# Mixture-of-experts layer: weighted slot results added by accumulating gathers, and a last shared phase that turns its inner rows through DRAM

## What is computed

```python
scores = softmax(xt @ Wg.T)                      # 16 experts, 4 groups; the best 2 groups stay
topi = top_k(masked, 4)                          # 4 experts a token
weights = take_along_axis(scores, topi)
h = silu(xt @ W1[e].T) * (xt @ W3[e].T)          # inner size 352
y = sum over e of (h @ W2[e].T) * weight of e
z = silu(xt @ Ws1.T) * (xt @ Ws3.T) @ Ws2.T      # shared expert, inner size 704
return y + z
```

## Time and profile before

| | |
|---|---|
| runs | 923.56, 919.63, 924.39 us, median 923.56 |
| span of the profiled execution | 919.3 us; no time of its own is listed beside it |
| last shared phase | about 810 to 919 us of the span |
| granted TensorE clock | 0.998 of full speed over the span |
| moved by DMA | 218.97 MB, 238 GB/s over the span |

### The profile page before, as it was taken

How to read it: one execution, slowest core, us unless ns; L and a number is a source line. 1 busy time by engine, 2 the same in 40 slices (tenths; PEclk the granted TensorE clock), 3 DMA queues, 4 the chain that set the end, 5 groups by cost and what they waited for, 6 DMA issues and landing times.

```text
span 919.3 us, 19365 instructions
## 1 busy us (share of the span) xinstructions
PE 899.9 (98%) x4962; PEld 806.1 (88%) x4963; DVE 557.9 (61%) x1105; ACT 332.0 (36%) x708; POOL 494.3 (54%) x346
## 2 busy tenths in 40 slices
PE   8999998899989999999999999999999999999998
PEld 5777887687889999999999999999999999989997
DVE  6656767888896644544444444444444444459997
ACT  4556554354324322333333333333333333332221
POOL 1127777874167764434646664456666643136772
PEclk9999999999999999999999999999999999999999
DMA  6829996665569956878778776788777755588984
GB/s 214 264 106 385 388 403 251 230 189 172 184 227 297 308 206 207 243 205 247 245 235 252 248 246 203 237 244 258 248 251 249 248 170 158 163 231 241 275 254 144
DMA packets 180649, 218.97 MB, mean 238 GB/s; under 512 B 56576, under 2 KB 124160, under 8 KB 180224
## 3 DMA queue, kind: packets, MB, share of 16 engines
q1 hardware_dynamic: 118080, 123.49, 41.9%
q0 software_dynamic: 20816, 79.44, 26.1%
q10 hardware_dynamic: 41712, 15.54, 6.3%
HBM read 127.38 MB, written 91.03 MB: 238 GB/s over the span
## 4 chain that ended last, share of the span: by engine, by line
PE 80%; DVE 9%; issue 4%; ACT 3%; DMA 3%; ACTq 0%; DVEq 0%; POOL 0%; SPq 0%; POOLq 0%
PE ps L1170 15%; PE ps L1171 15%; PE ps L1172 15%; PE ps L1222 8%; PE ps L1224 8%; PE ps L1223 8%; PE ps L1019 2%; PE ps L1035 2%; PE ps L966 1%; DVE st L1469 1%; DVE res L1467 1%; PE ps L1055 1%; PE ps L1057 1%; PE ps L1056 1%; DVE st L1284 1%
## 5 line engine op out<-in xcount | busy, mean ns | idle before, releaser
L1170 PE MATMUL ps<-whi,xhi 128*128 (+1 forms) x888 | 288.8, 325 | 1.2 <-issue 0.6
L1172 PE MATMUL ps<-whi,xlo 128*128 (+1 forms) x888 | 286.7, 323 | 0.0
L1171 PE MATMUL ps<-wlo,xhi 128*128 (+1 forms) x888 | 286.7, 323 | 0.0
L1544 DVE TENSOR_TENSOR hrow<-ps,sg 128x352 f32<-128x352 f32 x95 | 49.7, 523 | 214.1 <-ACT sg L838 214.1
L1170 PEld LDWEIGHTS ps<-whi,xhi 128*128 128x128 f32 x888 | 167.7, 189 | 6.1 <-issue 1.3
L1171 PEld LDWEIGHTS ps<-wlo,xhi 128*128 128x128 f32 x888 | 167.7, 189 | 3.9
L1172 PEld LDWEIGHTS ps<-whi,xlo 128*128 128x128 f32 x888 | 167.3, 188 | 0.0
L838 ACT ACTIVATE sg<-ps 128x352 f32<-128x352 f32 x111 | 51.5, 464 | 268.1 <-PE ps L1172 268.0
L845 ACT ACTIVATE xhi<-ps 128x512 fp32r<-128x512 f32 x112 | 66.9, 597 | 145.8 <-DVE ps L1505 145.7
L566 POOL TENSOR_TENSOR wlo<-raw,whi 128x2816 fp32r<-128x2816 f32 x16 | 100.7, 6291 | 2.4 <-POOL whi L564 0.9
L658 POOL DMA_INDIRECT raw<-yslot_d,sloti x64 | 67.7, 1058 | 57.7 <-DMA yslot_d<-ysb 22.6
(11 more groups left out here) (201 smaller groups left out, 1583.4 us busy)
## 6 DMA issues: line engine op xcount, KB each, us to landing
raw<-wexp_in POOLq DMA_DIRECT2D x18, 2176.0 KB, 11.1
xslot_d<-zero SPq DMA_DIRECT2D x10, 2048.0 KB, 21.6
xg<-xslot_d SPq DMA_DIRECT2D x320, 64.0 KB, 2.8
yslot_d<-ysb SPq DMA_DIRECT2D x80, 256.0 KB, 2.4
h_d<-hrow ACTq DMA_DIRECT2D x79, 192.0 KB, 3.0
hblk<-h_d SPq DMA_DIRECT2D x79, 192.0 KB, 2.5
xg<-xn_d SPq DMA_DIRECT2D x128, 64.0 KB, 3.7
xq<-x_in SPq DMA_DIRECT2D x16, 256.0 KB, 3.3
```

The costliest lines, as they stand in the source:

```text
L1170: pe.matmul(ps[:, bank, 0:INTER], xh, wh, start=(k == 0), stop=False)
L1171: pe.matmul(ps[:, bank, 0:INTER], xh, wl, start=False, stop=False)
L1172: mm = pe.matmul(ps[:, bank, 0:INTER], xl, wh, start=False, stop=(k == KT - 1))
```

## The change

It has three parts.

1. **Weights move into the slots.** The softmax over all 16 experts is worked out at the start of the first shared phase (`prob`). Rows of xslot_d grow from 512 to 528 numbers (SROW): the scattered row carries the token's 16 probabilities, brought into `scat` by a second small load. In the expert phase SP loads the 16 probabilities of each tile's slots (`load_w`), and ScalarE's `y_evac` scales by the column of the tile's expert, which it reads from the packed table, so that yslot_d holds weighted results.
2. **Gathers accumulate.** The 64 gathers of the last phase have `compute_op=ALU.add` and go to x1 directly. They are ordered in four groups of four tiles, choice by choice; each waits for the previous choice of its tile. gath, `combine` and the semaphore comb go. `add_last` stands one step later and waits for all four gathers of its tile.
3. **Last shared phase as expert tiles.** Tiles 0 to 14 store the inner row to h_d (`store_last_h`), load it (`load_last_h`) and turn it on VectorE (`last_h_turn`); the down product is two tiles behind. Tile 15 alone is still transposed by TensorE (`tr_last_h`). The gate product alternates between two PSUM banks here too, and the phase is written out without a loop. The weights of the second shared half are laid out as the experts' are; for tile 15 VectorE writes the inner row in that order by two instructions.

```diff
+SROW = D + E
-LAG, PACE = 1, 9
-        xslot_d = nc.dram_tensor("xslot_d", [NR * P, D], F32, kind="Internal").ap()
+        xslot_d = nc.dram_tensor("xslot_d", [NR * P, SROW], F32, kind="Internal").ap()
         def gate_bank(base, p):
-            return 7 if base == NT and p else 2
+            return 7 if base >= NT and p else 2
...
             def load_scat(t, r, turn):
-                sp.dma_start(scat[:, r, :], rows(xn_d, t)).then_inc(scat_loaded[r], 16)
+                sp.dma_start(scat[:, r, 0:D], rows(xn_d, t)).then_inc(scat_loaded[r], 16)
+                if type(t) is not int or t >= XR:
+                    sp.dma_start(scat[:, r, D:SROW], prob[:, bass.ds(t, 1), :]).then_inc(scat_loaded[r], 16)
+                elif t == XR - 1:
+                    sp.wait_ge(rt_prob, 1)
+                    for i in range(XR):
+                        sp.dma_start(scat[:, i, D:SROW], prob[:, i, :]).then_inc(scat_loaded[i], 16)
...
+            def load_w(t, r, turn):
+                if type(t) is int and t == NR - 1:
+                    return
+                if type(t) is not int or t >= XG:
+                    sp.wait_ge(y_out, 2 + NT + t - XG + 1)
+                sp.dma_start(wslot[:, r, 2:2 + E], rows(xslot_d, t)[:, D:SROW]).then_inc(w_loaded[r], 16)
...
-            stream(sp, [(NR, True, [(-1, load_h), (XG + 1, load_slots), (-3, store_y)], None),
-                        (NT, False, [(0, None), (XG + 1, load_tile(NT + NR, xn_d)), (-4, store_out)], None)], XG)
+            stream(sp, [(NR, True, [(-1, load_h), (XG + 1, load_slots), (-3, store_y), (1, load_w)], None),
+                        (NT, False, [(-1, load_last_h), (XG + 1, load_tile(NT + NR, xn_d)), (-5, store_out), (0, None)], None)], XG)
...
-            for t in range(NT):
-                if 1 <= t < GR:
-                    pool.wait_ge(gathered[t - 1], 16 * TOPK)
-                if t >= GR:
-                    pool.wait_ge(mm1, 2 + NT + NR + t - 2)
-                    pool.wait_ge(comb, TOPK * (t - GR + 1))
+            for first in range(0, NT, GR):
                 for k in range(TOPK):
-                    pool.indirect_dma_start(
-                        out=gath[:, t % GR, k, :], out_offset=None, in_=yslot_d,
-                        in_offset=bass.IndirectOffsetOnAxis(ap=sloti[:, t * TOPK + k:t * TOPK + k + 1], axis=0)).then_inc(gathered[t % GR], 16)
+                    for t in range(first, first + GR):
+                        if first or k:
+                            pool.wait_ge(gathered[t % GR], 16 * TOPK * (t // GR) + 16 * k)
+                        pool.indirect_dma_start(
+                            out=x1[:, t, :], out_offset=None, in_=yslot_d,
+                            in_offset=bass.IndirectOffsetOnAxis(ap=sloti[:, t * TOPK + k:t * TOPK + k + 1], axis=0),
+                            compute_op=ALU.add).then_inc(gathered[t % GR], 16)
...
-                act.activation(ysb[:, p, :], ps[:, 5 + p, :], ACT.Copy).then_inc(y_out, 1)
+                act.wait_ge(w_loaded[r], 16 * (turn + 1))
+                act.activation(ysb[:, p, :], ps[:, 5 + p, :], ACT.Identity, scale=wslot[:, r, bass.ds(expert(t, r), 1)]).then_inc(y_out, 1)
...
-                         (NT, True, [(0, by_two(silu_g(NT + NR))), (0, None), (-1, by_two(h_high(NT + NR))), (2, by_two(x_high(NT + NR))), (0, None), (0, None)], None)], XG)
+                         (NT, False, [(0, by_two(silu_g(NT + NR))), (0, store_last_h), (0, None), (2, by_two(x_high(NT + NR))), (-2, by_two(h_high(NT + NR))), (0, None)], None)], XG)
...
-                        (NT, True, [(0, tr_h(NT + NR)), (-1, down(NT + NR, last)), (2, up(NT + NR, last))], None)], XG)
+                        (NT, False, [(-1, tr_last_h), (-2, down(NT + NR, last)), (2, up(NT + NR, last))], None)], XG)
...
+            r_shifted()
             dve.wait_ge(h_pad, 1)
             h_mult(0)(0, 0, 0)
...
             x_turn(0)(2, 2, 0)
+            r_softmax()
...
             def add_last(t, r, turn):
                 p = r % 2
                 dve.wait_ge(mm2, NT + NR + t + 1)
-                if issued["comb"]:
-                    dve.wait_ge(comb, issued["comb"])
+                dve.wait_ge(gathered[r], 16 * TOPK * (turn + 1))
...
-                         (NT, False, [(0, h_row(NT + NR)), (0, combine(0)), (0, None), (2, x_turn(NT + NR)), (-1, h_low(NT + NR)), (0, combine(1)),
-                                      (2, x_low(NT + NR)), (-2, add_last), (0, combine(2)), (0, combine(3))], None)], XG)
+                         (NT, False, [(0, h_row(NT + NR)), (0, None), (0, None), (2, x_turn(NT + NR)), (-2, last_h_turn), (2, x_low(NT + NR)),
+                                      (-2, h_low(NT + NR)), (-3, add_last)], None)], XG)
```

More of the change, by code:

```diff
@@ L322, in xattn_moe @@
         gathered = [sem(f"gathered{r}") for r in range(GR)]
-        comb = sem("comb")
+        w_loaded = [sem(f"w_loaded{r}") for r in range(XG)]
         out_stored = [sem(f"out_stored{p}") for p in range(2)]
@@ L409, in fn @@
                     sp.wait_ge(x_tr, base + t + 1)
-                    blocks = rows(src, t).rearrange("(c i) (q n) -> i q c n", i=Q, q=NQ)
+                    blocks = rows(src, t)[:, 0:D].rearrange("(c i) (q n) -> i q c n", i=Q, q=NQ)
                     for q in range(NQ):
@@ L873, in _ @@
             silu_g(0)(0, 0, 0)
+            act.wait_ge(rt_low, 1)
+            act.activation(prob[:, :, :], prob[:, :, :], ACT.Exp).then_inc(rt_exp, 1)
             def h_high(base):
@@ L888, in h_high, with load_words, expert, y_evac @@
                 return fn
-            def y_evac(t, p, half):
+            words = []
+            def load_words(j):
+                words[:] = [act.value_load(packed[0:1, bass.ds(j, 1)], min_val=0, max_val=32 ** XG - 1)]
+            def expert(t, r):
+                if type(t) is int:
+                    return act.value_load(order[0:1, t:t + 1], min_val=2, max_val=E + 1)
+                return words[0] // 32 ** ((r + 2) % XG) % 32
+            def y_evac(t, r, turn):
+                p, half = r % 2, 2 * turn + r // 2
+                if type(t) is int and t == 0:
+                    act.wait_ge(rt_done, 1)
                 act.wait_ge(mm2, NT + t + 1)
@@ L913, in second_high, with silu_again @@
                         first_high(1)(i, p, half)
-            def exponents(t, p, half):
-                if type(t) is int and t == 5:
-                    act.wait_ge(rt_low, 1)
-                    act.activation(score[:, :, :], score[:, :, :], ACT.Exp).then_inc(rt_exp, 1)
-                    act.activation(top8f[:, :, 0:TOPK], top8f[:, :, 0:TOPK], ACT.Exp).then_inc(rt_exp, 1)
+            def silu_again(t, p, half):
+                if type(t) is int and t == 0:
+                    act.activation(silu_warm[:, :], const[:, C_EPS:C_EPS + 1], ACT.Silu).then_inc(warm, 1)
             def expert_high(t, p, half):
@@ L1160, in fn @@
                     for m in halves:
-                        if base == NT and m:
+                        if base >= NT and m:
                             pe.wait_ge(h_ready, base + t)
@@ L1233, in fn, with tr_last_h @@
                     pe.wait_ge(h_lo, base + t)
-                    transposes(ps[:, 4, :], hrow[:, p % 2, :] if base else hx[:, :], IC, h_tr)
+                    transposes(ps[:, 4, :], hx[:, :], IC, h_tr)
                 return fn
+            def tr_last_h(t, r, turn):
+                if t < NT - 1:
+                    return
+                pe.wait_ge(h_ready, NT + NR + t + 1)
+                pe.wait_ge(h_lo, NT + NR + t)
+                transposes(ps[:, 4, :], hrow[:, r % 2, :], IC, h_tr)
             words = []
@@ L1775, in _ @@
             x_turn(0)(2, 2, 0)
-            issued = {"comb": 0, "y_out": 2 + NT}
+            r_softmax()
             def add_last(t, r, turn):
@@ L1786, in add_last @@
                 dve.tensor_tensor(x1[:, t:t + 1, :], x1[:, t:t + 1, :], ps[:, 5 + p:6 + p, :], ALU.add).then_inc(y_out, 1)
-                issued["y_out"] = 2 + NT + NR + t + 1
-            def combine(quarter):
-                def fn(s, r, turn):
-                    begin, end = (max(0, min(TOPK * NT, ((4 * u + v) - 4 * LAG) * PACE // 8)) for u, v in ((s, quarter), (s, quarter + 1)))
-                    for n in range(begin, end):
-                        t, k = n // TOPK, n % TOPK
-                        if k == 0:
-                            dve.wait_ge(gathered[t % GR], 16 * TOPK * (t // GR + 1))
-                        dve.wait_ge(y_out, issued["y_out"])
-                        if n:
-                            dve.wait_ge(comb, n)
-                        dve.scalar_tensor_tensor(x1[:, t:t + 1, :], gath[:, t % GR, k:k + 1, :], top8[:, t:t + 1, k],
-                                                 x1[:, t:t + 1, :], ALU.mult, ALU.add).then_inc(comb, 1)
-                        issued["comb"] += 1
-                return fn
             def first_row(t, r, turn):
```

80 lines of the change are left out of this document (52 added, 28 removed).

## The result

The changed kernel takes 951.37 us (median of five runs, 949.67 to 958.45) against 923.56: 1.0325 times as long, interval 1.0288 to 1.0361. That is slower, close to the 955.0 forecast and inside the range.

What follows compares the result with a forecast made beforehand. TensorE bounds the old kernel, DMA engines the changed last shared phase. Span 919.3 - 6.5 (TensorE) + 37.9 (gathers end last) = 950.7, plus 4.3 from span to time: 955 us; range 914 to 988.

Steps and rivals of the forecast that it cites:

- TensorE's gain of 0.43 us a tile: Last shared phase: 15 of 16 tiles run as expert tiles do, without PE transposes, 6.5 us less.
- The tail does not grow: End of last shared phase: tile 15's work unchanged, one more down product covers its latency; nothing added.
- Price of an adding gather: Last shared phase: 21.6 engine-us each against 14.4 plain, by bytes, half as much again; bounds 14.4 and 28.8.
- the rival of two passes: Last shared phase: both operands pass the DMA engine in turn, 28.8 engine-us a gather, 986 us; chance 0.18.
- 94% as the most that the DMA engines give: Last shared phase: busy share taken from the scatters' stretch, making 138.8 us of DMA work last 147.6 us.
- The mechanism: Last shared phase: full DMA engines make gathers end last, +37.9 us; VectorE waits for gathers at additions, TensorE gets holes.
- the change doesn't do what it says: Last shared phase: rival of inner rows waiting for their round trip, only with full DMA engines; counted inside the forecast.
- POOL's pace no longer sets the rate: Last shared phase: a round of four gathers lasts one landing plus 0.3 us of issue; POOL's time 5 us a round.
- forecast idle time of 4 us a round: Last shared phase: sign that POOL stands idle some 4 us in each round of gathers.
- Expert phase at 0 (0 to 5): Expert phase: weight load and longer slot rows cost nothing, or 0 to 5 us if weight-load bursts exceed the cover.
- First shared phase at 0 (at worst +2): Front of first shared phase: the early softmax fits into existing waits, 0 in all, at worst +2 us.
- From span to time: Whole kernel: 4.3 us added to the span, as the earlier runs' median lies above the profiled span.

Runs made afterwards that it cites:

- pe_turn: Changed kernel with the last shared phase's inner rows transposed by TensorE and the down product one tile behind, as before, adding gathers kept; 938.12 us, ratio 1.0180.
- half_adds: Changed kernel with only two of each tile's four adding gathers (32 in all), the other two choices missing from the output; 935.58 us, ratio 1.0150.
- no_gathers: Changed kernel with no gathers and no wait for them in the final addition, routed part missing from the output; 923.13 us, ratio 1.0017.
- turn_only: Kernel before with only the last phase's inner rows turned through DRAM and VectorE; plain gathers, weighted and added by VectorE; 929.78 us, ratio 1.0077.
- plain_gathers: Changed kernel with its 64 gathers not adding, written to a buffer in the same order with the same waits; 925.30 us, ratio 1.0027.

## Why the prediction was right, point by point

- **TensorE's gain of 0.43 us a tile: right.** Tile 95 to 110 went from 93.9 to 86.6 us without gathers, 7.3 us for 15 tiles where 6.5 was forecast. In the changed kernel the same stretch takes 106.7, so the gain is buried under the waits.
- **"The tail does not grow": wrong.** Without any gather the stretch from tile 110 to the end went from 9.7 to 12.5 us, and to 20.8 with the adding ones. The forecast had every tile's latency covered by a down product and overlooked that tile 14's round trip is on the path once the up products are over.
- **Price of an adding gather: right in kind, 8% low.** 23.6 engine-us, forecast 21.6. The second read, from which the price was worked out, is seen in no view. The Trainium skill (Collectives: The Full Stack, "The bandwidth ceiling: the fold count and why AG ≠ RS ≠ AR") states its rule for reduce-scatter in a ring; applied here it would have doubled the plain price. The traces have 23.6 / 14.4 = 1.64, so the rival of two passes, 986 us, fell.
- **94% as the most that the DMA engines give: wrong.** The share was 1.09 to 1.13 for 120 us. The measured work from 800 us on, gathers 1512 and hardware queues 977 engine-us (29.7% and 9.2%), is 269 more than the 2220 forecast (a part of the hardware queues' 139 more are expert tiles that now lie inside the window). A first gather 11.9 us later than forecast (811.78), a stretch to the last landing of 134.5 us instead of 147.6, and 10.6 us behind that landing instead of 3.2: 950.7 + 11.9 - 13.1 + 7.4 = 956.9. The hit of the total is owed in good part to errors that cancel.
- **The mechanism: half right.** That DMA work of the adding gathers decides, and that TensorE gets holes, was right. That the damage comes as gathers ending last, with VectorE waiting at the additions of tiles 4, 8 and 12, was wrong for this kernel: 0.5 us of such waits, and the chain does not end with a gather. It is right for pe_turn, at those very tiles. So 13.1 of the 25.9 us of the last phase are the gathers' late stream, as forecast, though POOL's pace has most part in it, and 12.8 came by the inner rows' round trip, which the forecast had folded into its rival "the change doesn't do what it says" and priced at nothing of its own. half_adds shows the error in the reasoning: the loss accrues while gathers run and needs no overrun at the end (over no_gathers 15.2 us with 32 of them, 30.1 with 64; of this 13.5 and 20.1 in tiles 95 to 110, the rest at both ends).
- **POOL: missed.** "POOL's pace no longer sets the rate", with the plain gather's 0.95 us. Issue takes 1.54 us; rounds lasted 8.06 us (126.9 us for 63 gathers, times four), 7.4 of them issue and its gaps (four times 1.85). With the old inner rows POOL's pace is nearly the whole bound. The forecast idle time of 4 us a round was 1.9 (8.06 less four times 1.54).
- **Expert phase at 0 (0 to 5): its upper bound.** 5.3 us at the first tiles behind the scatters (the mean of the changed kernel and those seven others is 28.1, against 22.8). The cover named, x tiles five ahead, doesn't bear on it: VectorE waits there for the hidden block, whose load stands in SP's order among the loads with which it catches up. The sign named, a span unchanged within 2 us up to 790 us, failed: tile 94 starts 11.7 us later (817.7 against 806.0).
- **First shared phase at 0 (at worst +2): right on average.** Tile 18 starts at 356.1 to 361.2 us in the ten kernels with the new softmax place, on average at 358.3, against 357.8 before; three of them, the changed kernel with +3.4 among them, lie beyond +2.
- **From span to time** the forecast added 4.3 us; the profiled execution has 958.45 - 956.9 = 1.6.

## What to carry to other kernels

Before work moves from a busy vector engine into a DMA, price the DMA on three counts: its engine time, what the issuing engine pays for each one, and how long every other transfer then takes to land. A round trip through DRAM that just fits its cover at a normal queue stalls as soon as the queue is deeper, even where the sum over the phase has room, so compare landing time with cover moment by moment. And two changes that share a resource must be priced together: here the turn through DRAM cost 7.7 us of the last phase beside plain gathers and VectorE's additions (turn_only, 121.0 against 113.3) and 12.8 beside adding ones, and without any gather or addition it gained 4.2 (109.1).

## What was unexpected of the hardware

- Issuing an adding gather of 128 rows of 2 KB holds POOL for 1.54 us against 0.95, and makes 144 packets (9216 / 64) against 80.
- It needs 23.6 engine-us against 14.4 (25.4 in pe_turn, 75.2% of 135 us on 16 engines; a plain one 13.8 in plain_gathers), with no more bytes counted, so GB/s (246 to 252 against 292 to 333) falls at a full share. That the difference is the second operand's reading, which the view does not count, is likely and was not shown.
- A DMA share over 1 (up to 1.13) is possible in this view; 0.94 was not a ceiling.
- TensorE's clock, granted at 1.00 in the windows of the earlier trace rows, was granted at 0.57 on average from 940 to 948 us and at 0.52 from 948 to 951.5, near its lower level of 1.2 GHz, after it had waited repeatedly for VectorE (1.27 us before a matmul at 935.68, 2.09 before one at 940.13, 3.32 before the transposes at 946.90). The three transposes of the chain took 0.87 us there against 0.33. Holes in TensorE's work so cost more than their own length.
